# Cross attentions of a four-layer decoder: scores computed in both orientations instead of transposed probabilities

## The reference, cut to what matters

```python
q, k, v = x @ Wq + bq, ctx @ Wk + bk, ctx @ Wv + bv      # L1: no biases
s = einsum("bhqd,bhkd->bhqk", q, k) / 4
s = clip(s, -10000, 10000)             # L0 only
s = where(mask, s, -max)               # L1 only
o = einsum("bhqk,bhkd->bqhd", softmax(s), v)
y = o @ Wo + bo                        # L3: relu(o @ W1 + b1) @ W2 + b2
```

## Time and profile before

| | us |
|---|---|
| median of 3 runs | 1798.14 |
| lowest and highest | 1793.85, 1798.26 |
| profiled execution | span 1785.6 (no other time is given for it) |
| L0 cross attention, first score to last row turned | 155.9 to 345.0 |
| L1 | 659.0 to 838.6 |
| L3 | 1351.7 to 1546.8 |

### The profile page before, as it was taken

One profiled execution on the slowest core, in us unless ns is written; L12 is line 12 of the kernel. 1 busy time (PEld: TensorE's weight loads), 2 busy tenths in 40 slices (PEclk: granted clock), 3 DMA queues, 4 the chain that ended last, 5 costly groups with the idle time before them and its releaser, 6 DMA issues.

```text
span 1785.6 us, 40853 instructions
## 1 busy us (share of the span) xinstructions
PE 1579.5 (88%) x14786; PEld 1305.9 (73%) x14786; DVE 941.3 (53%) x2546; ACT 717.5 (40%) x1675; POOL 409.0 (23%) x627
## 2 busy tenths in 40 slices
PE   7998998799987879998797788997988999899998
PEld 6876776678975657776687566775876777689897
DVE  3665877511116657777110562556345667565864
ACT  3334876232323336652222314551755556211110
POOL 2224776500004421112000233432121111000101
PEclk9998999999998999998899798998998999999999
DMA  5343000278951011102686001001001000033232
GB/s 212 147 151 121 28 27 19 106 279 300 321 185 35 1 53 44 29 15 87 254 290 228 13 1 58 28 27 48 1 1 66 23 26 15 24 96 117 81 108 68
DMA packets 41852, 166.72 MB, mean 93 GB/s; under 512 B 5985, under 2 KB 16865, under 8 KB 30177
## 3 DMA queue, kind: packets, MB, share of 16 engines
q1 hardware_dynamic: 39392, 159.14, 25.7%
q0 software_dynamic: 2304, 5.51, 1.0%
HBM read 140.21 MB, written 24.41 MB: 92 GB/s over the span
## 4 chain that ended last, share of the span: by engine, by line
PE 70%; DVE 12%; issue 7%; DMA 3%; POOL 3%; ACT 3%; SPq 1%; DVEq 0%; POOLq 0%; ACTq 0%
PE bank L1688 7%; PE bank L1701 6%; PE bank L1268 6%; PE bank L1630 4%; PE bank L1255 4%; PE bank L1631 4%; PE bank L1632 4%; PE bank L1282 3%; PE bank L795 2%; PE bank L804 2%; PE bank L1238 2%; PE bank L1243 2%; PE bank L896 1%; PE bank L782 1%; DMA xrow<-slots 1%
## 5 line engine op out<-in xcount | busy, mean ns | idle before, releaser
L2053 ACT ACTIVATE arena<-big,nm 112x375 f32<-112x375 f32 x384 | 215.9, 605 | 29.5 <-DVE nm L2894 16.4
L1268 PEld LDWEIGHTS bank<-cst,arena 112*125 112x125 f32 x1152 | 146.6, 192 | 54.0 <-issue 29.0
L1268 PE MATMUL bank<-cst,arena 112*125 112x112 f32 x1152 | 168.0, 283 | 8.8 <-ACT big L2063 5.0
L3150 POOL TENSOR_TENSOR mv<-mv,cst 112x1 f32<-112x1 f32 x88 | 20.1, 228 | 607.3 <-DVE mv L2283 607.3
L2202 ACT ACTIVATE htile<-bank,wup 128x128 f32<-128x128 f32 x280 | 79.7, 368 | 189.7 <-PE bank L1688 189.6
L1688 PE MATMUL bank<-xtile,wup 128*128 128x128 f32 x1120 | 132.8, 278 | 0.3 <-DVE xtile L2997 0.2
L1688 PEld LDWEIGHTS bank<-xtile,wup 128*128 128x128 f32 x1120 | 129.8, 194 | 1.0 <-DVE xtile L2997 0.9
L3013 DVE COPY yrow<-bank 128x256 f32<-128x256 f32 x35 | 14.8, 424 | 217.5 <-PE bank L1701 217.5
L1701 PE MATMUL bank<-wdn,htile 128*128 128x256 f32 x560 | 126.3, 379 | 0.0
L2897 DVE TENSOR_SCALAR_CACHE_REDUCE big<-bank 112x375 f32<-112x375 f32 x192 | 96.0, 543 | 35.3 <-PE bank L1255 33.6
L1701 PEld LDWEIGHTS bank<-wdn,htile 128*128 128x128 f32 x560 | 103.9, 190 | 12.8
(11 more groups left out here) (359 smaller groups left out, 3571.7 us busy)
## 6 DMA issues: line engine op xcount, KB each, us to landing
wup<-in_moe_up SPq DMA_DIRECT2D x35, 1028.0 KB, 7.3
wdn<-in_moe_dn SPq DMA_DIRECT2D x35, 1024.0 KB, 6.1
vspace<-in_ring SPq DMA_DIRECT2D x40, 512.0 KB, 4.2
ctxs<-parts SPq DMA_DIRECT2D x30, 564.0 KB, 3.9
slots<-mlpw SPq DMA_DIRECT2D x11, 1024.0 KB, 6.5
parts<-ctxs SPq DMA_DIRECT2D x8, 564.0 KB, 3.1
xrow<-slots SPq DMA_DIRECT2D x35, 128.0 KB, 5.0
slots<-yrow SPq DMA_DIRECT2D x35, 128.0 KB, 7.0
```

Source lines behind the costliest of these rows:

```text
L1268: mm = pe.transpose(bank[4 + (3 * g + t) % 2][0:KT, j * T:(j + 1) * T], c_pr[:, g, j, t * KT:(t + 1) * KT], ident[0:T, 0:T])
L2053: nc.scalar.activation(c_pr[:, g, j, :], c_sc[:, g % 2, j, :], ACT.Exp, bias=nm[:, p, h:h + 1], scale=-1.0).then_inc(cexp_done, 1)
```

## The change

A class `Joined` and `cross_joined` on each engine take the place of `cross`. Keys are stored four times over (`m_kT`): per head of the pair, with the other head's rows zero but for one row of ones; queries likewise on plain rows (`m_q`). A round is four banks of six, in turn. In an S round PE makes the scores of four heads, 112 x 375, and DVE only takes their maxima, two banks per instruction (L1: one fused add and maximum per head). The 16 maxima are turned by two transposes (`maxima`) and subtracted from the queries' free rows (`queries_less`), giving `m_q2`. In a T round PE makes the scores of all 16 heads again with keys in partitions, 125 x 448 per bank, the maxima already taken off by the row of ones, and ACT takes the exponential of two banks at once straight to SBUF as the operand of `values`. L0 has one more T round (`least`) with the lower bound of each query; DVE clamps the exponentials with it (`clipped`).

Removed: POOL's `spread` and `clip`, PE's 48 transposes per sequence, ACT's and DVE's copies of turned tiles, DVE's copies of scores. The work on a sequence is spread over four steps: S rounds in step b, T rounds in b+1 (`back`), values and output in b+2 (`o`), last rows in b+3 (`late`). Queries, keys and value rows now all pass through bank OT. The loop is unrolled. POOL's `prepare` (biases with masks) is queued before the self attention ahead of each of these cross attentions.

PE's order in L0 (`step_clipped`), with S and T rounds named by number: g0: S0, second keys of b, `least`; g1: S1, `values`, `rows_t`, T of piece 0, value rows 0, `output_rows`; g2: S2, `output_columns`, value rows 1, T of piece 1, value rows 2; g3: S3, `project_out`, first keys of b+1, T of piece 2, `q_in` of b+1, `maxima`. ACT follows the same order. DVE's in L0: g0: maxima S0, `clipped(o, 2)`, `rows_out`; g1: maxima S1, output copy and scaling; g2: maxima S2 with `output_columns` between, `clipped(back, 0)`; g3 as below.

```diff
+        self.turns, self.tops = (4, 17) if clip else (3, 16)
+        self.rounds = []
+        order = "S0 T0 S1 T1 S2 T2 S3 T3" if clip else "S0 T0 S1 T1 S2 S3 T2"
+        for b in range(B + 1):
+            for kind, x in order.split():
+                if kind == "S" and b < B:
+                    self.rounds.append(("S", b, int(x)))
+                if kind == "T" and b:
+                    self.rounds.append(("T", b - 1, int(x)))
...
+        def round_banks(sub, r):
+            return [bank[(4 * r + j) % 6] for j in range(4)]
...
+        def round_pairs(sub, r):
+            return [banks[:, (4 * r + 2 * i) % 6:(4 * r + 2 * i) % 6 + 2, :] for i in range(2)]
...
+                def taken(r, n):
+                    kind, b, x = sub.rounds[r]
+                    if kind == "R":
+                        pe.wait_ge(route_in, 6 * nr + b + 1)
+                    elif kind == "S":
+                        pe.wait_ge(mx_done, sub.top(b, 4 * x + n))
+                    else:
+                        pe.wait_ge(me_done, 4 * sub.turned(b, x) + n)
+                def room(r):
+                    if r >= 2:
+                        taken(r - 2, 4)
+                    if r >= 1:
+                        taken(r - 1, 2)
+                def scores(b, c):
+                    r = sub.round_at["S", b, c]
+                    if c == 0:
+                        pe.wait_ge(cq_done, at(sub, "c1", b, 1))
+                        if b:
+                            pe.wait_ge(mq_done, first + b)
...
+                    room(r)
+                    for j, to in enumerate(round_banks(sub, r)):
                         rows = slice(32 * j, 32 * j + 32)
+                        mm = pe.matmul(to[0:T, 0:S2], m_q[rows, b % 2, c, :], m_kT[b % 3][rows, c, :], start=True, stop=True)
+                    mm.then_inc(ms_ready, 1)
...
+                def scores_t(b, t):
+                    r = sub.round_at["T", b, t + sub.clip]
                     if t == 0:
+                        pe.wait_ge(mq_done, first + b + 1)
+                    room(r)
+                    for c in range(4):
+                        for j, to in enumerate(round_banks(sub, r)):
+                            rows = slice(32 * j, 32 * j + 32)
+                            mm = pe.matmul(to[0:KT, c * T:(c + 1) * T], m_kT[b % 3][rows, c, t * KT:(t + 1) * KT], m_q2[rows, c, :],
+                                           start=True, stop=True)
+                    mm.then_inc(mt_ready, 1)
+                def maxima(b):
+                    pe.wait_ge(mx_done, sub.top(b, sub.tops))
+                    to = turned_maxima(sub, b)
+                    for e in range(2):
+                        mm = pe.transpose(to[:, e * T:(e + 1) * T], m_max[:, e, :], ident[0:T, 0:T])
+                    mm.then_inc(mm_ready, 1)
+                def values(b):
+                    pe.wait_ge(me_done, 4 * sub.turned(b, sub.turns))
+                    if sub.clip:
+                        pe.wait_ge(md_done, 6 * b + 6)
+                    pe.wait_ge(cv_done, at(sub, "c3", min(b + 1, B - 1), 3))
+                    pe.wait_ge(cot_in, at(sub, "t1", b, 0))
+                    pe.wait_ge(v_zero, 2)
+                    for g in range(GROUPS):
+                        for t in range(3):
+                            for j in range(4):
+                                h = head_of(g, j)
+                                mm = pe.matmul(OT[32 * j:32 * j + 32, g * T:(g + 1) * T], vbuf[:, b % 2, t, 32 * h:32 * h + 32],
+                                               m_p[:, t, j, g * T:(g + 1) * T], start=(t == 0), stop=(t == 2))
+                    mm.then_inc(mv_ready, 1)
...
-                def transposes(b, g, p, t):
...
-                        mm = pe.transpose(bank[4 + (3 * g + t) % 2][0:KT, j * T:(j + 1) * T],
-                                          c_pr[:, g, j, t * KT:(t + 1) * KT], ident[0:T, 0:T])
-                    mm.then_inc(ct_ready, 1)
...
+                def step(b, g, now, back, o, late):
+                    more = b + 1 < B
+                    if now is not None:
+                        scores(b, g)
                     if g == 0:
+                        if o is not None:
+                            values(o)
+                        if late is not None:
+                            rows_t(sub, late, late % 2)
+                        if back is not None:
+                            scores_t(back, 0)
+                        if o is not None:
+                            if late is not None:
+                                pe.wait_ge(xt_done, xt_at(sub, late))
+                            output_rows(sub, o)
+                        if now is not None:
+                            if o is not None:
+                                pe.wait_ge(cot_in, at(sub, "t1", o, 1))
+                            elif b:
+                                pe.wait_ge(cv_done, at(sub, "c3", b - 1, 3))
+                            value_rows(b, 0, OT)
+                    if g == 1:
+                        if o is not None:
+                            output_columns(sub, o)
+                        if now is not None and b:
+                            pe.wait_ge(cv_done, at(sub, "c3", b, 1))
+                            keys(b, 1, OT)
+                        if back is not None:
+                            scores_t(back, 1)
+                        if now is not None:
+                            pe.wait_ge(ck_done, at(sub, "c2", b, 2))
+                            pe.wait_ge(cv_done, at(sub, "c3", b, 1))
+                            value_rows(b, 1, OT)
+                        if o is not None and sub.mlp:
+                            hidden(o)
+                    if g == 2:
                         if more:
+                            pe.wait_ge(cv_done, at(sub, "c3", b, 2))
+                            keys(b + 1, 0, OT)
+                        if o is not None:
+                            project_out(o)
+                    if g == 3:
+                        if more:
+                            pe.wait_ge(ck_done, at(sub, "c2", b + 1, 1))
+                            q_in(b + 1, OT)
+                        if back is not None:
+                            scores_t(back, 2)
+                        if now is not None:
+                            if more:
+                                pe.wait_ge(cq_done, at(sub, "c1", b + 1, 1))
+                            else:
+                                pe.wait_ge(cv_done, at(sub, "c3", b, 2))
+                            value_rows(b, 2, OT)
+                            maxima(b)
...
+                    for e in range(2):
+                        ins = nc.scalar.activation(m_kT[b % 3][:, 2 * m + e, :], src[:, 0:S2], ACT.Identity,
+                                                   bias=m_bias[:, 4 + 2 * m + e:5 + 2 * m + e], scale=w(sub, "plainmask")[:, e:e + 1])
+                    ins.then_inc(ck_done, 1)
...
+                def exps(b, t):
+                    if first + b:
+                        act.wait_ge(mv_ready, first + b)
+                    act.wait_ge(mt_ready, sub.turned(b, t + sub.clip + 1))
+                    for i, src in enumerate(round_pairs(sub, sub.round_at["T", b, t + sub.clip])):
+                        bias = {"bias": m_mask[:, 3 * b + t:3 * b + t + 1]} if sub.mask else {}
+                        nc.scalar.activation(m_p[:, t, 2 * i:2 * i + 2, :], src[0:KT, :, 0:4 * T], ACT.Exp, **bias).then_inc(me_done, 2)
+                def least(b):
+                    if b:
+                        act.wait_ge(md_done, 6 * b)
+                    act.wait_ge(mt_ready, sub.turned(b, 1))
+                    for i, src in enumerate(round_pairs(sub, sub.round_at["T", b, 0])):
+                        nc.scalar.activation(m_low[:, 2 * i:2 * i + 2, :], src[0:KT, :, 0:4 * T], ACT.Exp, bias=c("floor", KT)).then_inc(me_done, 2)
...
+                    if g == 3:
+                        if more:
+                            keys(b + 1, 0, OT)
+                            q_in(b + 1, OT)
+                        if back is not None:
+                            exps(back, 2)
...
+                        dve.reduce_max(to.rearrange("p j n -> p (j n)"), src[0:T, :, 0:S2], AX_X).then_inc(mx_done, 2)
...
+                def clipped(b, t):
+                    for i in range(2):
+                        js = slice(2 * i, 2 * i + 2)
+                        dve.wait_ge(me_done, 4 * sub.turned(b, t + 1) + 2 * i + 2)
+                        dve.scalar_tensor_tensor(out=m_p[:, t, js, :], in0=m_p[:, t, js, :], scalar=1.0, in1=m_low[:, js, :],
+                                                 op0=ALU.min, op1=ALU.max).then_inc(md_done, 1)
+                def queries_less(b):
+                    dve.wait_ge(mm_ready, first + b + 1)
+                    dve.tensor_tensor(m_q2.rearrange("p (m e) n -> p m e n", m=2),
+                                      m_q[:, b % 2, :, :].rearrange("p (m e) n -> p m e n", m=2),
```

(32 more changed lines are left out.)

824 lines of the change are left out of this document (419 added, 405 removed).

## The result

The changed kernel took 1849.8 us, median of four runs (1847.6 to 1851.0), the kernel before 1798.2 (1793.9 to 1798.8): a ratio of 1.030, 95% interval 1.027 to 1.032. The forecast was 1785.5 and its range ended at 1822, so sign and range were both wrong. Every execution on record took some 2 us more than its span (1.7 to 2.1), so the profiled execution of before took, by estimate, 1787.5 us: it was one of the quickest, and about 11 of the 63.5 us are that.

What follows compares the result with a forecast made beforehand. PE was taken to bound all three cross attentions. L1 -12.6, L3 -17, L0 +16 and start +1 gave -12.6: span 1773.0, with the median 12.5 above it 1785.5 us; own range 1765 to 1792, 8 in 10 runs 1742 to 1822.

Steps and rivals of the forecast that it cites:

- PE's part: PE's slots per step: 48 transposes (5.4 us) go, three 1.03 us rounds come; sums 16.6 (L1), 17.7 (L0), 19.5 (L3).
- the readers: ACT's and DVE's two-bank passes, about 0.92 and 0.93 us; neither engine's sum reaches PE's.
- the second rival below: PE's sum carries through with only today's 1.5 us of waits per step: some 1744 us; chance 0.25.
- the walk: One step of each stage followed product by product with its waits: 19.2 us in L1, 24.25 in L0, 21.0 in L3.
- L0's walk: L0's step, with S1 waiting for `least` and S0 for ACT: 24.25 us against 20.5, +3.7.
- rival 2: Slower: PE's clock falls in L0; half its slots at half clock add 62 us, 1848; chance 0.31 with its kin.
- Ends of the stages: First steps and drains of the three stages; after the last S3 27.5 us in L1, 30 in L3, 33 in L0.
- L1's steps: L1's first two steps 28.5 us, then five of 19.2; its stage with routing 167, -12.6.
- Start: Before L0: POOL's `prepare` waits for the second pack and delays its copies of x; L856 near 19.2, +1 us.
- Between the stages: Experts' first weights wait as before; L3's first ring pieces 0, at worst 4 us.
- A1: Theory after the measurement: the loss is the waits, with L0's walk and the ends too short.
- A2: Theory after the measurement: the waits also lower PE's clock, and that is most of the loss.

## Why the prediction was wrong

- **PE's part and the readers**: right. The steps of L1 and L3 at full clock are 19.0 and 20.9 us for 19.2 and 21.0, ACT's and DVE's two-bank passes 0.917 and 0.936. (What the prediction calls "the second rival below", PE's sum, is the first in its list.) One pass was priced low: a key pass has both a bias column and a scale column now and took 0.660 us for 0.569; it lay beside PE's work in the walk.
- **L0's walk**: right as far as it went. With PE's clock held and the waits left alone the step was 24.2 for 24.25, and the waits are the ones named.
- **The clock in L0, the term left out of the sum.** It stood as rival 2, which shared 0.31 with its kin. The rival had place, cause and sign right: a stretch empty before S1 in every step, walked as 3 us, measured as 1.5 to 2.8. Its size was 62 us over seven steps, for half of the slots at half clock; the runs showed 16 over the stage (237.9 to 221.9), since the clock came back within each step. That its 1848 us lies so near the measured 1849.8 is luck: the rest of that distance is the ends below and POOL. What failed is the choice: the sum took L0's step at full clock while it wrote down a 3 us gap in each, and the earlier trace rows had the doubled product before it.
- **Ends of the stages, with the clock the largest error in the sum.** The walk's numbers from the last query product to the last turned rows (its 3.2 and 4.3 us from a query to its S0 added, L1's for L3), and what was measured, in us:

| | L0 | L1 | L3 |
|---|---|---|---|
| walked | 55 | 46.8 | about 50 |
| changed kernel | 71.7 | 65.8 | 57.6 |
| gaps filled (L0, L1); last values at full clock (L3) | 66.3 | 59.3 | 56.0 |
| of this POOL's queue | 4.1 | 1.6 | 0 |
| walked too short by | 7 | 11 | 6 |
| of the third row, less POOL's: from the last values' start | 11.4 | 14.9 | 15.9 |
| the same in the trace of before | 11.9 | 11.0 | 14.5 |

  Most of what is missing lies behind the last values, where the walk had 7.6 us (19.9 to 27.5 in L1). The same chain of copy, transposes, division, transposes, projection, norm and turned rows was in the trace of before. Its last values were only 48, 24 and 24 products there where 96 stand now (24 took 0.71 us, 96 take 2.51), so it gave, by estimate, near 13, 13 and 16 us; the walk did not look at it. In L1 the 11 us hold DVE's routing too, 2.99 us in one wait before the second turned scores, where the walk allowed 2 in all.
- **Added up**: the ends were walked 24 us too short in the three stages together, and the clock is worth about as much: 16 in L0's stage and 1.7 more in its drain, some 4 in L1, 1.5 in L3.
- **L1's steps**: its first two took 32.5 us for 28.5 and the next five 99.4 for 96. The second alone took 21.6; in nine other traces with the new form in L1 it took 19.0 to 20.3. So 1 to 3 of these 7 us are this one execution's.
- **POOL's queue**: not in the prediction at all. Its last transfers moved ahead of the norm's root and cost 4.1 us in L0's last wait and 1.6 in L1 (1849.8 to 1843.5 in the medians). The rule to count each queue that a step is moved past would have found it.
- **Start**: +1 predicted, for POOL's `prepare` ahead of its copies of x; L938, the former L856, starts 1.7 later, at 19.98 us, but not for that reason. PE reaches it without a wait, and the products ahead of it took 6.91 us for 5.45. In six other traces of kernels with this same start they took 5.40 to 5.62, and there PE waits 0.25 to 0.45 us for POOL's copy of x and starts at 18.8 to 19.3, near the 19.2 walked. The +3.9 at L0's first scores is mostly scatter: in the eight traces of kernels with this same start they begin at 155.2 to 159.8 us, against 155.9 before, and from L0's first query product to them it is 3.14 us for 2.96.
- **Between the stages** +7.2 and -5.0 us were measured where 0 was predicted. From L1's end to L3's first scores the thirteen traces here take 508.2 to 516.6 us, so the -5.0 is scatter. From L0's end to L1's first scores it is 314.6 before and twice 316.4 with L1 in its old form, 318.8 to 321.7 in ten traces with the new: some 4 us go with L1's new form, and what makes them was not tried.

The step of the prediction that failed, then, is twofold: L0's step was put into the sum at full clock in spite of the gap that the walk itself showed, and the drains of all three stages were walked too short. For L0, 16 us of the 49 are what the walk gave, 16 the clock, 4 POOL's queue, and of the 12 to 13 that remain some 9 are the too short end (1.7 of them clock again), the rest steps a little longer than walked. Both theories hold, each for its part: A1 for two thirds, A2 for one.

## What to carry to other kernels

An engine's sum, even a walk of its waits, is not a step time on PE if the walk leaves it idle for 2 to 3 us in a step: price the first few us of work behind such a gap at half clock in the sum itself (half of the whole step was four times too much here), or fill the gap. A stage with eight steps is start and drain for a good part; take its last chain, from the last product to the last result, from the trace of before and not from a walk. When one form serves three places, time it in each alone: here the form that gains 7 us in the last layer went in together with one that lost 49 in the first and one that cost some 11 in the second. And one profiled execution is one draw: stretches that no edit touched differ by up to 8 us between two traces here.

## What the runs showed of the hardware

A gap of 1.29 us before S1 and one of 2.25 before S0 in a step let the clock fall in one step and not in the next of the same kernel; in the changed kernel 2.25 before S0 and 1.5 to 2.8 before S1 lowered it in every steady step of L0, to 0.78 to 0.93 over the step, and with fillers that left 0.44 and 0.50 it stayed at 1.00.

With L0 in its old form and L1's gaps filled PE stood 1.41 us in the middle of a round of turned scores in L1 (L1642), where no wait in the code can be, and then ran at half clock for 4 us (value rows L1586 1.42 us for 0.86, scores L1619 1.42 for 0.90):

```profile
762.25 0.57 PE L1642 MATMUL banks<-arena,big 32*125 32x112 f32 x9
764.23 0.99 PE L1642 MATMUL banks<-arena,big 32*125 32x112 f32 x23 [1.41 <-issue]
765.16 1.10 PE L884 MATMUL banks<-cst,arena 128*112 128x128 f32 x4
765.91 1.42 PE L1586 MATMUL banks<-kv,ctxs 128*125 128x256 f32 x5
767.26 1.42 PE L1619 MATMUL banks<-big,arena 32*112 32x375 f32 x8
```

That step took 22.1 us for 19.0, and the one before it as much, with a stand of 1.91 us behind the same round. Without L1's fillers, which come later in the program, the two stands are there too, 1.41 us after the same ninth product and 1.93 behind the same round: they go with the place in the program. In the changed kernel and in the one with POOL's transfers late the stand is at another place, 1.29 and 1.49 us before the same value rows. The new form is written out step by step where the old one loops; the Trainium skill, Runtime: NRT & Kernel Launch, section Instruction fetch mechanics, says that a sequencer fetches its code in blocks by DMA while it runs and that the crossing is mostly hidden. Such a fetch would fit the 1.41 us, but no run here tests it.
